# Attention b written out step by step, its causal mask moved from TensorE to VectorE, and three quarters of the second FFN's preparation placed inside its steps

## What is computed

```python
x = x + attn_a(_layernorm(x), ...)   # log-sparse attention, 16 heads of 8
x = x + ffn(_layernorm(x), ...)      # 8 experts, each token goes to the one with the largest affinity
x = x + attn_b(_layernorm(x), ...)   # causal attention, 16 heads of 64
x = x + ffn(_layernorm(x), ...)      # the same experts again

# attn_b
scores = jnp.where(tril(ones), K @ Q, NEG_INF)
attn = softmax(scores / sqrt(64))
out = concat_heads(V^T attn) @ W_O^T

# ffn
aff = x @ centroids.T
assign = argmax(aff, axis=1)             # sort the tokens by expert
alpha = sigmoid(aff[assign])
h = relu(layernorm(xs) @ w1[e].T + b1[e])
ye = xs + h @ w2[e].T + b2[e]
out = alpha * ye + (1 - alpha) * xs      # and put them back in place
```

## Time and profile before

| what | value |
|---|---|
| time, median of 3 runs | 582.73 us (582.52 to 586.84) |
| the profiled execution's own time | 583.51 us |
| its span in the profile | 581.7 us |
| PE busy | 466.7 us, 80% |
| DVE busy | 370.0 us, 64% |
| ACT busy | 229.2 us, 39% |
| POOL busy | 235.5 us, 40% |
| attention b's steps | about 205 to 482 us from the span's start |
| preparation of the second FFN | 482 to 524 us |
| slots of the second FFN | 524 to 573 us |

### The profile page before, as it was taken

How to read it: one execution, slowest core, us unless ns; L and a number is a source line. 1 busy time by engine, 2 the same in 40 slices (tenths; PEclk the granted TensorE clock), 3 DMA queues, 4 the chain that set the end, 5 groups by cost and what they waited for, 6 DMA issues and landing times.

```text
span 581.7 us, 10958 instructions
## 1 busy us (share of the span) xinstructions
PE 466.7 (80%) x3500; PEld 367.0 (63%) x3500; DVE 370.0 (64%) x1090; ACT 229.2 (39%) x835; POOL 235.5 (40%) x245
## 2 busy tenths in 40 slices
PE   3957994608986299999999999999999964509993
PEld 2323663508985167787878778787877754409893
DVE  6599877734574477757675775667577527635672
ACT  2710003303442056636554663655466333304441
POOL 5003883562444234434243443424344324552443
PEclk9979997557999599999999999999999977558997
DMA  9999400126462200000000000000000000126560
GB/s 319 402 422 420 204 1 1 49 99 183 120 193 74 64 0 2 1 2 1 0 0 0 0 0 0 0 0 0 0 0 1 0 2 1 63 98 183 140 201 23
DMA packets 21861, 47.50 MB, mean 82 GB/s; under 512 B 3233, under 2 KB 13480, under 8 KB 19394
## 3 DMA queue, kind: packets, MB, share of 16 engines
q1 hardware_dynamic: 18818, 40.73, 20.3%
q0 software_dynamic: 3008, 6.34, 3.1%
HBM read 23.82 MB, written 24.15 MB: 82 GB/s over the span
## 4 chain that ended last, share of the span: by engine, by line
issue 79%; PE 15%; SPq 2%; DMA 2%; ACT 0%; POOLq 0%; POOL 0%; DVE 0%; ACTq 0%
PE ps L820 7%; PE ps L833 7%; PE ps L810 1%; DMA pv<-sorted_in 1%; DMA pv<-in_w 0%; DMA after_ffn<-pv,dest 0%; SPq L409 0%; SPq L357 0%; POOLq L142 0%; SPq L373 0%; SPq L370 0%; ACT pv L584 0%; DVE pv L1260 0%; SPq L376 0%; ACT pv L594 0%
## 5 line engine op out<-in xcount | busy, mean ns | idle before, releaser
L493 POOL TENSOR_TENSOR vT<-vT,prec 128x256 f32<-128x256 f32 (+1 forms) x128 | 103.2, 826 | 168.0 <-DVE prec L1321 168.0
L616 ACT ACTIVATE vT<-ps,nmax 128x128 f32<-128x128 f32 (+1 forms) x256 | 105.1, 434 | 26.0 <-DVE nmax L1313 26.0
L624 ACT COPY prod<-ps 128x384 f32<-128x384 f32 x96 | 42.9, 481 | 117.6 <-PE ps L920 114.2
L1313 DVE TENSOR_REDUCE nmax<-ps 128x2 f32<-128x256 f32 (+1 forms) x128 | 62.4, 550 | 33.9 <-PE ps L900 33.9
L865 PE MATMUL ps<-xnT,wb 128*128 128x256 f32 x256 | 67.0, 385 | 4.6 <-DVE xnT L1293 3.9
L920 PEld LDWEIGHTS ps<-cst,vT 128*128 128x128 f32 x384 | 44.7, 141 | 18.7 <-issue 15.8
L616 ACT ACTIVATION_READ_ACCUMULATOR vT<-ps,nmax 128x1 f32 x256 | 56.1, 219 | 0.0
L920 PE MATMUL ps<-cst,vT 128*128 128x128 f32 x384 | 52.5, 273 | 1.8 <-POOL vT L493 1.7
L933 PE MATMUL ps<-prod 128*64 128x256 f32 (+1 forms) x512 | 49.8, 337 | 3.1 <-ACT prod L624 2.1
L833 PE MATMUL ps<-w2s,pv 128*128 (+1 forms) x368 | 50.0, 279 | 2.0 <-issue 2.0
L894 PE MATMUL ps<-qk 64*128 64x128 f32 (+1 forms) x512 | 51.0, 338 | 0.0
(11 more groups left out here) (151 smaller groups left out, 829.9 us busy)
## 6 DMA issues: line engine op xcount, KB each, us to landing
sorted_in<-zero SPq DMA_DIRECT2D x1, 16512.0 KB, 58.5
pv<-in_w SPq DMA_DIRECT2D x30, 259.0 KB
pv<-sorted_in SPq DMA_DIRECT2D x46, 129.0 KB
wps<-in_w SPq DMA_DIRECT2D x1, 2072.0 KB, 9.2
w2s<-in_w SPq DMA_DIRECT2D x1, 2048.0 KB, 13.2
wb<-in_w_b SPq DMA_DIRECT2D x1, 1536.0 KB, 17.5
xres<-in_x SPq DMA_DIRECT2D x4, 256.0 KB, 3.8
xres<-after_ffn SPq DMA_DIRECT2D x4, 256.0 KB, 3.8
```

Source lines behind the costliest of these rows:

```text
L493: last = nc.gpsimd.tensor_tensor(px, px, view(prec, m_at(n, x) + t * 2, [[1, 2], [0, (t + 1) * P]]), ALU.mult)
L616: last = nc.scalar.activation(pb[:, o:o + (t + 1) * P], wide[:, c:c + (t + 1) * P], ACT.Exp, bias=nmax[:, m:m + 1], accum_out=psum[:, m:m ...
L624: nc.scalar.copy(pT[:, c:c + BLOCKS * P], bank[hh][:, 0:BLOCKS * P]).then_inc(b_pa, 1)
L1313: last = nc.vector.tensor_reduce(nmax[:, m:m + 2], view(wide, x * 1024 + t * P, [[512, 2], [1, (t + 1) * P]]), AX.X, ALU.max, negate=True)
```

## The change

Three things are changed at once.

**The loop is written out.** `all_steps` now calls `step` for every step with plain numbers. A step can so hold work of its own.

**The mask moves.** `mask_b`, the bf16 tiles and their setup are gone from TensorE and ScalarE. VectorE's maximum becomes eight `tensor_tensor_reduce` per step, one for each head and query tile: it reads the scores (PSUM) and a stretch of the constants (an open tile of zeros followed by the causal tile), adds them, negates, writes the result back over the scores and gives the row's minimum in `accum_out`. The exponential then has `scale=-1.0`. `invert(n, 1)` now stands behind the wait for the scores, `invert(n1, 0)` ahead of `copy_p`, and `copy_v` goes from VectorE to ScalarE, between `copy_p` and the second `exp_b`.

**Three groups of the second FFN are prepared in the steps.** Groups are now pairs of batches (`place_of`), so that group h can start when batches 2h and 2h+1 are done. `group_at(n)` gives the group h and a phase d = 0 to 7; steps 9 to 16 prepare group 0, 17 to 24 group 1, 25 to 32 group 2. Only group 3 is prepared after the last step. The maps in PSUM of affinities and ranks move to columns that the steps leave free.

```diff
-        def all_steps(eng, step, lead, tail):
-
-            for i in range(-lead, STEPS):
+        def all_steps(step, lead, tail):
+
+            for i in range(-lead, NB * STEPS + tail):
                 step(*at(0, i))
-            with eng.Fori(1, NB - 1) as b:
-                for j in range(STEPS):
-                    step(b, j)
-            for i in range(STEPS + tail):
-                step(*at(NB - 1, i))
+
+        def group_at(n):
+
+
+            return divmod(nth(n) - 2 * STEPS - 1, 2 * STEPS)
```

GpSimd:

```diff
-            all_steps(pool, divide, 0, 0)
-            ffn(1, out.rearrange("b l d -> (b l) d"))
+            def step(b, j):
+                n = (b, j)
+                divide(b, j)
+                h, d = group_at(n)
+                if 0 <= h < NG - 1 and d == 2:
+                    powers(1, h)
+                if 0 <= h < NG - 1 and d == 7:
+                    dispatch(1, h, [0])
+                if 1 <= h and d < GT - 1:
+                    dispatch(1, h - 1, [d + 1])
...
+            all_steps(step, 0, 0)
+            dispatch(1, NG - 2)
+            powers(1, NG - 1)
+            dispatch(1, NG - 1)
```

ScalarE:

```diff
                         last = nc.scalar.activation(pb[:, o:o + (t + 1) * P], wide[:, c:c + (t + 1) * P], ACT.Exp,
-                                                    bias=nmax[:, m:m + 1], accum_out=psum[:, m:m + 1])
+                                                    bias=nmax[:, m:m + 1], scale=-1.0, accum_out=psum[:, m:m + 1])
...
+                if some(bv) and j != 1 or some(b) and j == 1:
+                    copy_v(n, (j + 2) % STEPS)
                 if ok(n1):
                     exp_b(n1, 1)
-
-            all_steps(act, step, 1, 0)
+                h, d = group_at(n)
+                if 0 <= h < NG - 1 and d == 3:
+                    turned_v(1, h)
+                    residual(1, h)
+                if 0 <= h < NG - 1 and d == 5:
+                    exps(1, h)
```

TensorE (`step`, behind `project_qk(n2, 1)`):

```diff
                 if ok(n1):
                     scores_b(n1, 0)
                     scores_b(n1, 1)
-                    mask_b(0)
                 if ok(n):
                     turn_p(n, 0)
-                if ok(n1):
-                    mask_b(1)
...
+                h, d = group_at(n)
+                if 0 <= h < NG - 1 and d == 3:
+                    pe.wait_ge(b_pa, 3 * nth(n) + 3)
+                    turn_v(1, h)
+                if 0 <= h < NG - 1 and d == 4:
+                    pe.wait_ge(b_pd, nth(n) + 1)
+                    affinity(1, h)
+                if 0 <= h < NG - 1 and d == 6:
+                    pe.wait_ge(b_pd, nth(n) + 1)
+                    rank(1, h)
```

VectorE:

```diff
             def max_b(n, x):
-                dve.wait_ge(b_s, 2 * nth(n) + x + 1)
-                for t in range(T):
-                    m = m_at(n, x) + t * 2
-                    last = nc.vector.tensor_reduce(nmax[:, m:m + 2],
-                                                   view(wide, x * 1024 + t * P, [[512, 2], [1, (t + 1) * P]]),
-                                                   AX.X, ALU.max, negate=True)
+
+                for hh in range(2):
+                    for t in range(T):
+                        m, c, open_at = m_at(n, x) + t * 2 + hh, (2 * x + hh) * 512 + t * P, C_CAUSAL - t * P
+                        s = wide[:, c:c + (t + 1) * P]
+                        last = nc.vector.tensor_tensor_reduce(out=s, in0=s, in1=cst[:, open_at:C_CAUSAL + P], scale=-1.0,
+                                                              scalar=-MASKED * 2, op0=ALU.add, op1=ALU.min,
+                                                              accum_out=nmax[:, m:m + 1])
...
                     copy_z(at(b, j - 1))
+                if ok(n1):
+                    scored(n1)
                 if ok(n):
                     invert(n, 1)
                 if ok(n1):
                     max_b(n1, 0)
-                    max_b(n1, 1)
                 if ok(n2):
                     copy_qk(n2, 0)
-                if some(bv) and j != 1 or some(b) and j == 1:
-                    copy_v(n, (j + 2) % STEPS)
+                if ok(n1):
+                    max_b(n1, 1)
+                    invert(n1, 0)
                 if ok(n):
                     copy_p(n)
-                if ok(n1):
-                    invert(n1, 0)
...
+                h, d = group_at(n)
+                if 0 <= h < NG - 1:
+                    if d == 0:
+                        dve.wait_ge(b_x, 2 * h + 2)
+                        means(1, h)
+                    if d == 1:
+                        spread(h)
+                    if d == 2:
+                        norm(1, h)
+                    if d == 4:
+                        choose(1, h)
+                    if d == 5:
+                        count(1, h)
+                    if d == 6:
+                        place(1, h)
```

More of the change, by code:

```diff
@@ L194, in hybrid_layer @@
         zero = sb("zero", [P, 8 * ROW])
+        fmv = sb("fmv", [P, NT * 2])
         vv = sb("vv", [P, 2 * NT])
@@ L606, in ffn @@
                         normed(s + 2)
+            for g in range(NG + 1):
+                if g < NG:
+                    residual(0, g)
+                    turned_v(0, g)
+                if g > 0:
+                    exps(0, g - 1)
+            act.wait_ge(in_f, 4 * 16)
             ffn(0)
@@ new lines, in turn_v, with affinity @@
+            def turn_v(k, g):
+                pe.wait_ge(f_vh, k * NG + g + 1)
+                need(pe, f_vTs, k * NG + g)
+                for i in range(GT):
+                    t = g * GT + i
+                    last = nc.tensor.transpose(bank[k][:, i * P:(i + 1) * P], pack[:, t * ROW:t * ROW + D], ident)
+                last.then_inc(f_vT, 1)
+            def affinity(k, g):
+                pe.wait_ge(f_vTs, k * NG + g + 1)
+                for i in range(GT):
+                    c = aff_at[k][g] + i * NE
+                    last = nc.tensor.matmul(wide[:, c:c + NE], vTt[:, i * P:(i + 1) * P], cent_s[:], start=True, stop=True)
+                last.then_inc(f_aff, 1)
@@ L806, in turn_x, with totals @@
+            def totals(k):
+                pe.wait_ge(f_hs, (k + 1) * NG)
+                for h in range(NG):
+                    last = nc.tensor.matmul(wide[:, total_at:total_at + NE], ones_bf[:],
+                                            hsum[:, h * NE:(h + 1) * NE], start=h == 0, stop=h == NG - 1)
+                last.then_inc(f_total, 1)
+            def ffn(k):
                 def turn_x(s):
@@ L848, in ffn @@
                 output(NSLOT - 1)
+            pe.wait_ge(a_x, NU)
+            pe.wait_ge(in_r, 1)
+            pe.wait_ge(in_f, 4 * 16)
+            for g in range(NG + 1):
+                if g < NG:
+                    turn_v(0, g)
+                    affinity(0, g)
+                if g > 0:
+                    rank(0, g - 1)
+            totals(0)
             ffn(0)
@@ L965, in _ @@
             pe.wait_ge(b_w, 1)
-            all_steps(pe, step, 3, 1)
+            all_steps(step, 3, 1)
+            turn_v(1, NG - 1)
+            affinity(1, NG - 1)
+            rank(1, NG - 1)
+            totals(1)
             ffn(1)
@@ L1271, in ffn @@
                 finish(NSLOT - 1)
+            dve.wait_ge(a_x, NU)
+            nc.vector.tensor_copy(view(pack, 2 * D + 1, [[ROW, NT]]), cst[:, C_TOKEN:C_TOKEN + NT])
+            for g in range(2):
+                means(0, g)
+                spread(g)
+            for g in range(NG + 2):
+                if g < NG:
+                    norm(0, g)
+                if g + 2 < NG:
+                    means(0, g + 2)
+                    spread(g + 2)
+                if 0 <= g - 1 < NG:
+                    choose(0, g - 1)
+                    count(0, g - 1)
+                if 0 <= g - 2:
+                    place(0, g - 2)
+            tables(0)
             ffn(0)
@@ L1362, in _ @@
             dve.wait_ge(n_rs, 2)
-            all_steps(dve, step, 3, 1)
+            dve.wait_ge(f_sent, NT * 16)
+            nc.vector.tensor_copy(view(pack, 2 * D + 1, [[GT * ROW, NG], [2 * ROW, T], [ROW, 2]]),
+                                  view(cst, C_TOKEN, [[2, NG], [NB, T], [1, 2]]))
+            all_steps(step, 3, 1)
+            dve.wait_ge(b_x, NB)
+            means(1, NG - 1)
+            spread(NG - 1)
+            norm(1, NG - 1)
+            choose(1, NG - 1)
+            count(1, NG - 1)
+            place(1, NG - 1)
+            tables(1)
             ffn(1)
```

409 lines of the change are left out of this document (185 added, 224 removed).

## The result

The changed kernel takes 566.68 us (median of 4 runs, 562.9 to 569.77) against 582.92 (4 runs) beside it: a ratio of 0.969, with a 95% interval of 0.964 to 0.975. It is 16 us faster. The prediction had said 574 with a range from 568: the direction was right, the gain was 7 us too small, and the time lies 1.3 us under the range. The profiled execution took 566.59 us, its span is 564.8 against 581.7.

What follows compares the result with a forecast made beforehand. Each step was taken as a ring over TensorE, VectorE and ScalarE, closed after the change by ScalarE's copy of values. The terms 3.6+1.9+3.1+1.0+0.5-19.5 = -9.4 against 583.5 gave 574 us, range 568 to 604.

Steps and rivals of the forecast that it cites:

- The ring: One step's cycle from values to values through TensorE, VectorE and ScalarE; forecast to take 7.71 us, 7.40 before.
- The landmarks V+3.10 and V+4.69: Us after a step's first values matmul (V): VectorE starts its inversion; VectorE starts the copy of queries and keys.
- X: Time of a step's eight new maxima on VectorE: 2.8 us taken, bounds 2.7 and 4.05.
- ScalarE's chain, V+7.71: Exponentials, copy of probabilities, then the moved copy of values on ScalarE; ends last and lets the next values start at 7.71.
- VectorE's chain, V+7.54: Maxima, inversions and copies on VectorE; would let TensorE start the next values at 7.54 us.
- The sum of the batches: Four steps per batch: 34.41 us against 33.81, times six +3.6; the already unrolled batches +1.9.
- The preparation inside the steps: Three groups of the second FFN: affinity delays values by 0.83, rank adds 0.2, the rest hidden; +3.1 us.
- 3.1+1.0+0.5: Preparation of three groups in the steps, filling and draining the pipeline, and a possible VectorE stall meeting a chain, in us.
- The end: Behind the last step: last residual to first slot falls from 41.7 to 22 us; gain 19.5 us.
- The preparation is free and X at its lower end: Rival: step about 7.6 us, without the 3.1 and 1.5 us; 567 us; chance 0.10.
- The two rivals with a longer X: Read-outs don't overlap, X about 4.05, 604 us, chance 0.17; X 3.0 to 3.5, 581 us, chance 0.21.
- A stall by GpSimd's work: Rival: within the steps each of eight dispatches brings a VectorE stall of 3.9 us; +31, 605 us; chance 0.07.

Runs made afterwards that it cites:

- the moved dispatch: Against the kernel with both orders: in d = 2 GpSimd issues no dispatch behind the powers, it comes in d = 3; 559.44 us, ratio 0.958.
- both orders: Changed kernel with VectorE's copy of probabilities between heads of the second maxima and ScalarE's copies between heads of the first exponentials; 563.09 us, ratio 0.964.
- ScalarE's order alone: Changed kernel with ScalarE's copy of values and third copy of probabilities put between the first and last two exponentials of the first pair; 593.53 us.

## Why the prediction was right and wrong, point by point

**The ring, and that TensorE is not what ends a step: right.** The landmarks V+3.10 and V+4.69 came within 0.05, the step is set by copies on two other engines, and an instruction of 0.33 put ahead of VectorE's copy lengthened the step by 0.23, which is 0.33 less the slack within 0.02. The gap ahead of the values was 0.30, not 0.7 to 0.9; the granted clock stayed at 1.00 from 220 to 470, as forecast.

**The size of X: the step that failed, together with the exponentials of the next point.** "Lower bound X = 4x(0.21+0.33)+8x0.07 = 2.7", and 2.8 taken. Measured: 2.44, outside the bounds. The 0.07 per read-out was taken from two small VectorE instructions that stand behind each other; the read-out of an accumulator starts together with the next maximum and costs nothing. The slots without it, 0.21 to 0.25 and 0.38, even lie a little over my 0.21 and 0.33. So the term that made the "lower bound" was no bound: it rested on the assumption that a second instruction takes at least a slot. No row before the change told of a VectorE read-out; ScalarE's, the nearest, overlaps the exponential but still has 0.09 to itself.

**ScalarE's chain, V+7.71: the right chain, mis-sized.** It does close the ring, as forecast, at 7.38. 0.18 of the error is the first maxima (1.22, not 1.40), and 0.25 the exponentials: four took 1.60 (243.23 to 244.83), where I had read 1.85 from 457.74 to 459.59. In that stretch the copy of probabilities also waited 0.25 for its transposes. A duration read from one start to another holds the wait too. The copy of values and the start of TensorE behind it took 0.09 more than the 0.78 forecast. On VectorE's chain, V+7.54, only the second maxima count (0.18), since the copy ahead of them waits for TensorE; it ends at 7.30.

**What the two terms were worth.** With the measured maxima alone the prediction's own working gives a ring of 7.53 and some 569 us, inside the range; with the measured exponentials as well it gives 565 (see below, on the range). The miss needed both.

**The sum of the batches: wrong by about 7 us.** Forecast 34.41 a plain batch, measured 33.22, six of them: +3.6 against -3.5. In the written-out batches the forecast was +1.9; there too no step became longer. The loop was worth 0.29 of each batch and the mask 0.30, by the runs that changed one at a time.

**The preparation inside the steps: the mechanism right, the sum too low.** The affinity holds back the values, as said:

```profile
316.16 1.52 PE L963 MATMUL ps<-prod 128*64 128x256 f32 x16
...
323.40 1.06 PE L791 MATMUL ps<-cent_s,vTt 128*128 128x8 f32 x8 [0.15 <-DVE prod L1350]
324.31 0.42 PE L883 MATMUL ps<-cst,xn 128*128 128x128 f32 x2
324.66 1.52 PE L963 MATMUL ps<-prod 128*64 128x256 f32 x16
```

The affinity takes 1.06 (forecast 1.0), and the step is 8.50 (forecast 8.54), but that is 1.12 longer than 7.38 (forecast +0.83). It waits for the same copy of VectorE and so fills none of the gap, and the transposes of L883, which lie in the gap of a plain step, now stand behind it. The rank added 0.16 to 0.20 (0.2). What I had called hidden and was not: in two batches VectorE's `both` stood 1.78 for a four-column product, and these batches took 33.99 and 34.00, 0.77 more. The four batches with preparation cost 4.0 us together. With the last batch's 2.5 it is 6.5 against 3.1+1.0+0.5 forecast. Of the 2.5 some 0.9 are the lower clock of the last values and the last output projection (2.83 and 6.23, before 2.61 and 5.59), for which the forecast had no term.

**The end: right.** Residual to first slot 21.72, forecast 22; -20.0 against -19.5. The "remote" stall of VectorE did not come back in this stretch.

**The rivals.** "The preparation is free and X at its lower end", 567, gave the time but not the cause: X was under that lower end and the preparation was not free. I had given it 0.10 because I took two favourable cases to be needed at once. The two rivals with a longer X are refuted by the rows of L1361. A stall by GpSimd's work did exist, but at 0.8 in two batches instead of 3.9 at each of eight dispatches.

**The range.** Its low end left out what the term of X could do below 2.7. With the measured maxima and exponentials in the prediction's own working, the ring is 7.71-0.18-0.25 = 7.28 on ScalarE and 7.54-0.18 = 7.36 on VectorE, a batch 3x7.36+7.36+3.74 = 33.18, and the sum -3.8-0.2+4.6-19.5 = -18.9: about 565. The 1.9 that preparation, filling and draining cost beyond the forecast bring it to the 566.6 measured. That the time came out no further under the range is in part luck: the preparation was too small a term by 1.9 us, against the maxima and exponentials, which were too long.

## What to carry to other kernels

A lower bound built from "each instruction takes at least a slot" is none for an instruction that no row of the profile shows; let the low end of the range go to zero for it. When several chains release one instruction within a tenth, shortening one gains nothing there, and the name in the trace is not reliable: reorder each alone and together, and before moving an instruction list everyone who waits for it, not only the chain in mind. Before an experiment's gain is put down to its edit, take it apart by stretches: what lies where the edit does not reach is not its doing. A wait that covers two halves of the work is worth splitting once the ring runs over it.

## What the runs showed of the hardware

**The read-out of an accumulator.** On VectorE it starts in the same instant as the next maximum (244.24, 244.62, 244.87) and takes no slot, at 0.14 a record. The Trainium skill, "VectorE: DVE Perf Modes", section "The DRAIN you can't avoid", has the next instruction wait until the pipe is empty, and excepts one that is not held, by the section "Two Vector instructions with no wait between them". The slots of 0.21 to 0.25 under records of 0.29 and 0.33 agree with the exception, not with the rule.

**VectorE held up by GpSimd.** A product of two operands in SBUF, 128x4, took 0.16 in a quiet place and 0.72 and 1.78 in the steps, where it ended with GpSimd's division (the longest at 374.91, the division at 374.89). With the moved dispatch this product took 0.22 beside a running division, and the next one with two operands in SBUF, `shift`, took 1.00 and ended with the division. Why the first of them got through is open. By the Trainium skill, "SBUF — State Buffer", section "Who interferes with whom", a VectorE instruction with two SBUF inputs contends with a GpSimd instruction that reads SBUF; the traces agree. The maxima, with one input in PSUM, never showed it: the longest of 256 took 0.47.

**The clock in the drain.** While the pipeline empties, TensorE waits more. In the changed kernel its granted clock fell there from the 2.4 to the 1.2 GHz level; in the kernel with both orders and the moved dispatch it stayed up. Both in turn (columns: window, its length, busy time with counts of PE, PEld, DVE, ACT and POOL, granted clock, DMA share, GB/s):

```profile
472.00:484.00 12.00, 10.21 (x60) 8.59 (x61) 2.05 (x7) 0.48 (x1) 4.17 (x5) 0.57 0.14 45
```

```profile
470.00:479.00 9.00, 6.60 (x61) 5.59 (x61) 2.12 (x8) 0.83 (x2) 4.33 (x5) 1.00 0.13 45
```

The last output projection takes 6.23 in the one and 3.84 in the other:

```profile
478.09 6.23 PE L909 MATMUL ps<-wob,prod 128*128 128x128 f32 x32 [0.79 <-DVE prod L1346]
```

```profile
475.05 3.84 PE L911 MATMUL ps<-wob,prod 128*128 128x128 f32 x32 [0.79 <-DVE prod L1348]
```

With the last values (2.83 against 1.52) that is 3.7 us. What decides it is open. The waits of TensorE ahead of the drop were longer in the changed kernel (1.15 ahead of the last values but one and 1.75 ahead of the last transposes, against 0.70 and 1.06 in the one that kept its clock). But the kernel with both orders has these same 0.70 and 1.06, and its clock fell all the same:

```profile
471.21 2.46 PE L965 MATMUL ps<-prod 128*64 128x256 f32 x16
...
474.46 5.73 PE L911 MATMUL ps<-wob,prod 128*128 128x128 f32 x32 [0.79 <-DVE prod L1348]
```

So the length of these waits does not decide it. Between these last two kernels the clock makes 2.8 us, most of the gain measured with the moved dispatch. It was not a matter of one execution: the mean granted clock was 0.900 to 0.905 in the four of the one and 0.906 to 0.908 in the four of the other.

In the steps the clock fell too when the gaps grew: with ScalarE's order alone, at 1.0 us of gap in a step, it stood at 0.50 from 338 to 340, and the values and scores there took 2.57 and 2.15 instead of 1.52 and 1.58.
